# Normalizing the experts' mixture for eight tiles at a time, output gates carried in the record, second biases added while mixing

## The reference, cut to what matters

```python
xn = _layernorm(x)
# recurrent attention: 16 heads of 16 x 16 state
q, k = silu(xn @ Wq), l2_norm(silu(xn @ Wk)); v = xn @ Wv
f = sigmoid(xn @ Wf1 @ Wf2); a = k * (-sigmoid(xn @ Wgamma)) * f
for t in range(512):
    S = S * f_t; S = S + k_t * (a_t . S + v_t); o_t = q_t . S
o = o * sigmoid(xn @ Wog1 @ Wog2)          # the output gate
s = layernorm(o) * norm_w @ Wo
# experts: 2 of 8 for each token
y_e = gelu(xn @ W1[e] + b1[e]) @ W2[e] + b2[e]
g = silu(layernorm(sum_e cw[e] * y_e) * gamma + beta)
out = x + s * g
```

## Time and profile before

| | |
|---|---|
| median of 3 runs | 1239.27 us (1236.87 to 1240.11) |
| profiled execution, its own time | 1238.9 us |
| its span | 1237.2 us |
| busy: VectorE / TensorE / GpSimd / ScalarE | 90% / 76% / 74% / 32% |
| chain that ended last: GpSimd / VectorE / issue / TensorE / DMA | 36% / 27% / 16% / 7% / 6% |
| TensorE clock granted, mean | 0.869 of full speed |
| moved by DMA | 202.6 MB |

### The profile page before, as it was taken

The page is one execution under the profiler, slowest core; times in us unless marked ns, Lnnn a source line. Parts: engine busy times, 40 slices in busy tenths (PEclk is TensorE's granted clock), DMA queues, the critical chain, the costliest instruction groups (busy, mean ns, idle before and its releaser), DMA issues.

```text
span 1237.2 us, 17465 instructions
## 1 busy us (share of the span) xinstructions
PE 938.7 (76%) x3773; PEld 683.6 (55%) x3774; DVE 1119.4 (90%) x3502; ACT 395.7 (32%) x1047; POOL 918.9 (74%) x902
## 2 busy tenths in 40 slices
PE   5798898100029999999999999999999934667663
PEld 2343343000018888778888777888878723445441
DVE  3799999999999999999999999999999995988882
ACT  3444444200003333332232223333322203554552
POOL 3766666367844888888888888888888884877762
PEclk9888988655559999999999999999999976777787
DMA  5666656553335666655666556666666427355322
GB/s 165 194 209 177 213 180 188 140 191 107 111 94 150 191 196 195 195 170 183 191 195 193 174 177 195 196 187 181 183 192 191 120 67 210 93 157 149 99 81 69
DMA packets 247251, 202.60 MB, mean 164 GB/s; under 512 B 141425, under 2 KB 225233, under 8 KB 247185
## 3 DMA queue, kind: packets, MB, share of 16 engines
q1 hardware_dynamic: 170146, 82.81, 25.5%
q10 hardware_dynamic: 70224, 100.49, 24.8%
q0 software_dynamic: 6816, 18.69, 4.6%
HBM read 139.42 MB, written 62.54 MB: 163 GB/s over the span
## 4 chain that ended last, share of the span: by engine, by line
POOL 36%; DVE 27%; issue 16%; PE 7%; DMA 6%; SPq 3%; ACT 3%; POOLq 0%; DVEq 0%; ACTq 0%
POOL prod_q L327 13%; POOL prod_a L310 12%; POOL y_d L530 5%; DMA rec_d<-work 4%; DVE obh L1164 3%; PE psA L959 3%; DVE ubuf L1180 3%; DVE prod_a L1175 2%; PE psF L921 2%; SPq L335 2%; DVE prod_q L316 1%; DVE prod_a L1198 1%; DVE state L1204 1%; DVE outer L1190 1%; POOL cross L583 1%
## 5 line engine op out<-in xcount | busy, mean ns | idle before, releaser
L310 POOL TENSOR_TENSOR prod_a<-state,rbh 128x512 f32<-128x512 f32 x200 | 254.7, 1274 | 96.2 <-DVE state L1237 74.0
L903 PE MATMUL psF<-wts,work 128*128 128x256 f32 x1248 | 289.1, 385 | 3.2 <-ACT work L712 2.0
L891 PE MATMUL psA<-xgT,wts 128*128 128x256 f32 x1248 | 282.3, 384 | 0.9 <-ACT xgT L706 0.8
L891 PEld LDWEIGHTS psA<-xgT,wts 128*128 128x128 f32 x1248 | 235.4, 191 | 45.1 <-issue 13.8
L903 PEld LDWEIGHTS psF<-wts,work 128*128 128x128 f32 x1248 | 230.8, 190 | 50.0 <-issue 16.5
L327 POOL TENSOR_TENSOR prod_q<-state,rbh 128x512 f32<-128x512 f32 x175 | 223.2, 1276 | 0.0
L1164 DVE TENSOR_REDUCE obh<-prod_q 128x16 f32<-128x272 f32 x512 | 217.6, 426 | 0.0
L712 ACT ACTIVATE work<-psA,b_sb 128x256 f32<-128x256 f32 x312 | 130.8, 470 | 162.3 <-PE psA L891 159.5
L1224 DVE TENSOR_REDUCE ubuf<-prod_a 128x16 f32<-128x272 f32 x200 | 86.0, 430 | 37.5 <-POOL prod_a L310 37.1
L723 ACT ACTIVATE work<-psF,work 128x256 f32<-128x256 f32 x78 | 36.9, 473 | 256.9 <-PE psF L905 256.9
L879 PE MATMUL psT<-ident,work 128*128 128x128 f32 x156 | 24.2, 279 | 119.2 <-DMA work<-xs_d 119.1
(11 more groups left out here) (171 smaller groups left out, 1543.3 us busy)
## 6 DMA issues: line engine op xcount, KB each, us to landing
wts<-in_L_ffn_W_dram ACTq DMA_DIRECT2D x78, 1024.0 KB
rec_d<-work SPq DMA_DIRECT2D x32, 640.0 KB
rbh<-rec_d SPq DMA_DIRECT2D x32, 640.0 KB
xs_d<-zero SPq DMA_DIRECT2D x26, 387.0 KB, 9.0
work<-xs_d ACTq DMA_DIRECT2D x39, 258.0 KB
wts<-y_d ACTq DMA_DIRECT2D x16, 512.0 KB, 5.5
x_acc<-in_L_attn_x_dram SPq DMA_DIRECT2D x32, 128.0 KB
og_d<-work SPq DMA_DIRECT2D x32, 128.0 KB, 7.9
```

Source lines behind the costliest of these rows:

```text
L310: eng.tensor_tensor(prod_a[:, n, 1:3, :, 0:HD], state[:, g % SR, :, :].unsqueeze(1).broadcast_to(wide), rows.unsqueeze(2).broadcast_to(wid ...
L891: mm = pe.matmul(psA[m // 2 % 2][:, m % 2 * MT:(m % 2 + 1) * MT], w1_sb[v][:, c, m * P:(m + 1) * P], xgT[:, c, :], start=(c == 0), stop=(c ...
L903: pe.matmul(psF[q][:, 0:D], hT[:, m, q * P:(q + 1) * P], w2_sb[v][:, m, :], start=(m == 0), stop=False)
```

## The change

The record grows to 6 x 16 numbers: the output gate's sigmoids are written into it by one ScalarE instruction together with f. `og_d`, `ogs` and their DMAs go. A finished chunk of outputs is multiplied by its gates in `obh` (`gate_outputs`, 128x256): by VectorE for chunks 0 to 6 and 31, by GpSimd for chunks 7 to 30, behind pair 3 (GATED) of the next chunk; loads and stores of chunks wait for that. GpSimd's preparation moves from pairs 3 to 5 to pairs 4 to 6.

The b2 matmul leaves the expert tiles. Instead `route` forms each token's eight weights, TensorE turns them (into `cwT`), and `add_experts` begins each sum with a matmul of `cwT` and b2, which is held in four places (four small loads after a memset).

Mixing takes the moments of eight tile pairs ahead; `spreads` handles eight tiles (GQ) at once, four times in all, at places given by SPREADS; `moments` copies the sum to `x_acc`, so that the sum's PSUM is free before `normed`. ScalarE and TensorE finish the mixing of 24 tiles before the first output tile; the last eight alternate with output tiles 0 to 7. `out_scales` moves behind the next pair's products. LAND_STEP is 15.0 and PAIR_STEP 3.82.

```diff
-REC = 5 * HD
-A_, F_, K_, Q_, V_ = (HD * n for n in range(5))
+REC = 6 * HD
+A_, F_, O_, K_, Q_, V_ = (HD * n for n in range(6))
...
+GQ = 8
+SPREADS = (596.0, 608.0, 624.0, 650.0)
+GATED = 3
-LAND0, LAND_STEP = 390.0, 15.9
-PAIR_STEP = 3.7
+LAND0, LAND_STEP = 390.0, 15.0
+PAIR_STEP = 3.82
...
+        def gate_outputs(eng, c):
+            eng.tensor_tensor(obh[:, c % OB, :, :], obh[:, c % OB, :, :], rbh[:, c % RB, :, O_:O_ + HD], ALU.mult)\
+                .then_inc(s_og, 1)
...
-            sp.dma_start(b2_sb[:, :, :], b2.rearrange("(a e) n -> a e n", a=1)).then_inc(s_c, 16)
+            sp.wait_ge(s_pool0, 5)
+            for n in range(4):
+                sp.dma_start(b2_sb[n * E:(n + 1) * E, n, :], b2).then_inc(s_c, 16)
...
             def spill(n):
                 u4 = n % RS
-                sp.wait_ge(s_og, n + 1)
-                sp.dma_start(og_d[n], ogs[:, u4, :]).then_inc(s_ogd[u4], 16)
...
             def next_chunk(c):
-                sp.wait_ge(s_o, (c + 1) * RING)
+                sp.wait_ge(s_og, c + 1)
...
                 if n >= SL:
-                    sp.wait_ge(s_mul, n - SL + 1)
+                    sp.wait_ge(s_fb, n - SL + 1)
                 sp.dma_start(f_on[:, n % FR, :], o_r[n]).then_inc(s_fl[n % SL], 16)
-                sp.dma_start(fog[:, n % SL, :], og_d[n]).then_inc(s_fl[n % SL], 16)
...
-                if s % NP == 0:
+                if s % NP == GATED:
                     c = WOVEN + s // NP - 1
-                    sp.wait_ge(s_o, (c + 1) * RING)
+                    sp.wait_ge(s_og, c + 1)
...
-            def spreads(j):
-                lo, hi = 2 * j, 2 * j + 2
+            def spreads(q):
+                lo, hi = q * GQ, (q + 1) * GQ
...
-                if 3 <= g % NP < 6 and g // NP + 1 < NCH:
-                    prepare_part(g // NP + 1, g % NP - 3)
+                if g % NP == GATED and g // NP > SHARED:
+                    pool.wait_ge(s_o, g // NP * RING)
+                    gate_outputs(pool, g // NP - 1)
+                if 4 <= g % NP < 7 and g // NP + 1 < NCH:
+                    prepare_part(g // NP + 1, g % NP - 4)
                 s = g - WOVEN * NP
+                if spread < NT // GQ and ((g - SHARED * NP) * PAIR_STEP >= SPREADS[spread] or s >= 2):
+                    spreads(spread)
+                    spread += 1
                 if s >= 0:
                     for q, (lo, hi) in enumerate(NORMS):
-                        if s == hi - 1 and s < NT - 1:
+                        if s == hi:
                             out_scales(q)
...
-                    if s % 2 == 0:
-                        spreads(s // 2)
...
-                act.activation(rec[:, u4, :, F_:F_ + HD], heads(psF[u][:, 0:D]), ACT.Sigmoid).then_inc(s_f, 1)
-                act.activation(ogs[:, u4, :], psF[u][:, D:2 * D], ACT.Sigmoid).then_inc(s_og, 1)
+                act.activation(rec[:, u4, :, F_:F_ + 2 * HD].rearrange("p h (s c) -> p s h c", s=2),
+                               psF[u][:, :].rearrange("p (s h c) -> p s h c", s=2, h=H), ACT.Sigmoid).then_inc(s_f, 1)
...
-                    act.activation(junk[:, n % 2, :], summed(n), ACT.Copy, accum_out=ysum[:, n:n + 1]).then_inc(s_sum, 1)
+                    act.activation(x_acc[:, n, 0:D], summed(n), ACT.Copy, accum_out=ysum[:, n:n + 1]).then_inc(s_sum, 1)
...
-            moments(0)
-            for j in range(NT // 2):
-                normed(j)
...
+            half = GQ // 2
+            for j in range(2 * half):
+                moments(j)
+            for q in range(NT // GQ):
+                act.wait_ge(s_yr, q + 1)
+                for j in range(q * half, (q + 1) * half):
+                    normed(j)
+                for j in range((q + 2) * half, min((q + 3) * half, NT // 2)):
+                    moments(j)
+                for j in range(q * half, (q + 1) * half):
+                    silu_g(j)
+                    if q < NT // GQ - 1:
+                        if j > q * half:
+                            turned_back(j - 1)
+                    else:
+                        n = 2 * (j % half)
+                        out_normed(n)
+                        out_normed(n + 1)
+                        out_turned(n)
+                        turned_back(j)
+                        out_turned(n + 1)
+                if q < NT // GQ - 1:
+                    turned_back((q + 1) * half - 1)
+            for n in range(GQ, NT):
...
-                    pe.matmul(psF[q][:, 0:D], ones[0:1, :], b2_flat[:, bass.ds(e * D, D)], start=False, stop=True)\
-                        .then_inc(s_y, 1)
+                    mm.then_inc(s_y, 1)
...
                 if j >= 2:
-                    pe.wait_ge(s_yn, 2 * (j - 1))
+                    pe.wait_ge(s_sq, 2 * (j - 1))
                 for n in range(2 * j, 2 * j + 2):
+                    total = sums[j % 2][:, n % 2 * D:(n % 2 + 1) * D]
+                    pe.matmul(total, cwT[:, n // 4, :], b2_sb[:, n % 4, :], start=True, stop=False)
                     for c in range(2):
...
+                link(dve.tensor_tensor(gs[:, 2, :], gs[:, 2, :], gs[:, 0, :], ALU.mult))
+                dve.tensor_copy(x_acc[:, :, D], gs[:, 2, :]).then_inc(s_gate1, 1)
+                link(dve.tensor_tensor(pr, m1, over_e(2), ALU.mult))
+                link(dve.tensor_tensor(rest_, m2, over_e(4), ALU.mult))
+                dve.tensor_tensor(pr, pr, rest_, ALU.add).then_inc(s_cw, 1)
...
-                if out_tile is not None and out_tile < NT - 1:
-                    gate_o(out_tile)
...
+                    if n == GATED and 0 < c <= SHARED:
+                        dve.wait_ge(s_o, c * RING)
+                        gate_outputs(dve, c - 1)
```

More of the change, by code:

```diff
@@ L168, in build @@
         oTs = xTs
+        cwT = w_kq[0:4 * E, :, :].rearrange("p c n -> p (c n)").rearrange("p (n t) -> p n t", t=P)
         sel = gw[:, 0, :, :].rearrange("p t e -> p (t e)")
-        b2_flat = b2_sb[:, :, :].rearrange("a e n -> a (e n)")
         f_on = work[:, 0:FR * D].rearrange("p (u d) -> p u d", u=FR)
-        fog, fx, f_sg = (work[:, (FR + n * SL) * D:(FR + (n + 1) * SL) * D].rearrange("p (u d) -> p u d", u=SL)
-                         for n in range(3))
+        fx, f_sg = (work[:, (FR + n * SL) * D:(FR + (n + 1) * SL) * D].rearrange("p (u d) -> p u d", u=SL)
+                    for n in range(2))
         s_x = [sem(f"s_x{n}") for n in range(len(STATS))]
@@ L208, in build @@
         s_recd = [sem(f"s_recd{n}") for n in range(RS)]
-        s_ogd = [sem(f"s_ogd{n}") for n in range(RS)]
         s_gt = sem("s_gt")
@@ L220, in build @@
         s_b1t = sem("s_b1t")
+        s_cw = sem("s_cw")
+        s_cwT = sem("s_cwT")
+        s_cws = sem("s_cws")
         s_b1 = sem("s_b1")
@@ L398, in _ @@
                 sp.wait_ge(s_yd[u], 16 * MH * ((NM + 1 - u) // 2))
-            for u in range(RS):
-                sp.wait_ge(s_ogd[u], 16 * (NT // RS))
             def fetch(n):
@@ L591, in _ @@
             number(0)
-            landed = 0
+            landed = spread = 0
             for g in range(SHARED * NP, T // 2):
@@ L684, in _ @@
             act.wait_ge(s_b1, 1)
+            act.wait_ge(s_cwT, 1)
+            for n in range(2):
+                act.activation(cwT[:, 4 * n:4 * n + 4, :].rearrange("p n t -> p (n t)"), psA[n][0:4 * E, :], ACT.Copy)\
+                    .then_inc(s_cws, 1)
             act.wait_ge(s_slot, 2)
@@ L688, in _ @@
                 act.wait_ge(s_recd[u], 16 * (NT // RS))
-            for u in range(RS):
-                act.wait_ge(s_ogd[u], 16 * (NT // RS))
             def expert_of(t):
@@ L872, in _ @@
             pe.matmul(psT[1][:, 0:NT * E], ones[:, :], sel, start=True, stop=True).then_inc(s_cnt, 1)
+            pe.wait_ge(s_cw, 1)
+            for n in range(NT // 4):
+                mm = pe.transpose(psA[n // 4][0:4 * E, n % 4 * P:(n % 4 + 1) * P],
+                                  gw[:, 1, 4 * n:4 * n + 4, :].rearrange("p t e -> p (t e)"), ident[:, :])
+            mm.then_inc(s_cwT, 1)
             pe.wait_ge(s_slot, 2)
+            pe.wait_ge(s_cws, 2)
             def turn_rows(t, v, nth):
@@ L917, in add_experts @@
                 if j >= 2:
[L918 removed]
+                    pe.wait_ge(s_sq, 2 * (j - 1))
                 for n in range(2 * j, 2 * j + 2):
+                    total = sums[j % 2][:, n % 2 * D:(n % 2 + 1) * D]
+                    pe.matmul(total, cwT[:, n // 4, :], b2_sb[:, n % 4, :], start=True, stop=False)
                     for c in range(2):
[L921 to L922 removed]
+                        mm = pe.matmul(total, ident[:, :], yab[:, g % YR, c, n % GM, :], start=False, stop=(c == 1))
                 mm.then_inc(s_yab, 1)
@@ L960, in out_rows @@
                 mm.then_inc(s_s, 1)
-            add_experts(0)
-            for j in range(NT // 2):
-                if j + 1 < NT // 2:
-                    add_experts(j + 1)
-                turn_y(j)
-                turn_back(j)
-                if j > 0:
```

(16 more changed lines are left out.)

71 lines of the change are left out of this document (25 added, 46 removed).

## The result

The changed kernel takes 1296.65 us (median of four runs, 1295.98 to 1298.98), the kernel before 1239.69 beside it (1236.87 to 1241.72). The ratio is 1.046 (95% interval 1.044 to 1.049). The forecast had been 1221, range 1204 to 1238.

The account below looks back on a forecast made before the run. The recurrence's chain of waits between GpSimd and VectorE was taken as the bound. First sum at 978, plus 99 to tile 0, 111 and 5 of woven pairs, 26.5 tail and 1.7 around the span: 1221 us, range 1204 to 1238.

Parts of the forecast that it names:

- Front and experts: Stages before mixing: 57th pair 3 us later, expert tiles 14.9 us, pair pace 3.81 us, first sum at 978.
- A sum has 12 matmuls instead of 8: Mixing on TensorE: each tile pair's sum takes 2.8 us at 0.24 us per matmul, the first 4.4.
- rival B: Mixing: TensorE keeps the low clock, sums 5.4 us, tile 0 at 1122, end at 1266; chance 0.08.
- Turns: Mixing after the sums: silu, turn back and next turn take 2.7 us a tile pair at mean clock 0.70.
- seven spreads 4.8: VectorE's small operations for output groups in the woven pairs after tile 0: 0.7 us each, 4.8 in all.
- The 5 that I had left for late output tiles: Woven pairs: 5 us allowed for output tiles whose scales come just in time, bounds 0 and 16.
- one row of the front: Front gate products on VectorE: a 414 ns row taken to show no blocking by GpSimd; 2.4 us for seven.
- Waits: Woven stage: some 50 us of VectorE's waits can be had, including 17.1 us for gate tiles.
- a single wait at tile 0: VectorE, ready at 1060, waits 17 us for output tile 0, which comes at 1077.
- the tail: From the last state to the end: 26.5 us, against 27.1 before.

Follow-up runs that it names:

- e1: The changed kernel with the second-bias weights padded by zero rows from 32 to 128 rows; 1249.21 us, ratio 1.008 to the kernel before.
- e4: The changed kernel, 32-row bias weights kept, bias product first in even tiles and last in odd ones; 1257.95 us.
- e2: The changed kernel with the second-bias weights padded to 64 rows instead of 128; 1297.51 us.
- e9: e1 with output tiles started one group of eight sooner, output moments in PSUM and two-operand spread instructions reading one operand there; 1226.48 us, ratio 0.988.
- e10: e1 with GpSimd computing the output tiles' scales one pair earlier, as the kernel before does; 1243.04 us, ratio 1.003.
- e12: e9 with output tiles woven in from the seventh tile pair and the spread's last two all-SBUF operations reading one PSUM operand; 1211.87 us, ratio 0.975.

## Why the prediction was wrong, by its own steps

- **Front and experts: right in mechanism.** L905 has gone; the pace beside the experts is 154 pairs in 594 us from 386 on, 3.86 us (forecast 3.81). The last landing starts at 974.4 and the first sum at 982.7 (forecast 978). VectorE's waits for products there (386 to 960 us) are 22.3 us against 16.1 in the earlier trace rows: the densely placed landings cost somewhat more than I took.
- **The step that failed: "A sum has 12 matmuls instead of 8. At 0.24 us each (8 in 1.89) it takes 2.8 us."** It took 6.31. I priced the added products by a row of products whose weights are all 128 rows high, though the change makes them alternate with weights 32 rows high. The rows also held both ends, 1.89 and 3.62 for eight, and I kept the upper one only as rival B. The kernel before changes height too, around its second biases with weights of one row, and its weight loads stand idle there:

```profile
574.24 0.29 PEld L905 LDWEIGHTS psF<-b_sb,ones 1*128 1x128 f32 x2 [0.33 <-issue]
574.86 3.32 PEld L903 LDWEIGHTS psF<-wts,work 128*128 128x128 f32 x16 [0.33 <-issue]
```

So 0.62 us for two instructions, where two of 128 rows take 0.43 (e1), was a price on record. But it comes twice in 16 us and at a clock of 1.00, and nothing in it showed that the clock would stay low. The step is 15 x 3.5 = 52 us by itself; e1, in which only the heights are equal, has tile 0 49 us sooner.
- **Rival B had the place, not the cause.** B said 5.4 us a sum, tile 0 at 1122, end at 1266, with a chance of 0.08. The clock stayed low as B says, but I had it come from TensorE's rests, and argued it away with "TensorE would hardly rest while summing". It did not rest by the profile, 75.78 of 75.80 us, and the clock was 0.50. The Trainium skill (TensorE: Matmul & The Clock Gate, A second HAM failure mode: psum-queue depth-cycling) tells of a clock that goes back and forth where TensorE idles briefly between groups of matmuls. This trace agrees only in part: the weight loads idle 0.65 us at each change of height and e4, with half of the changes, has its high clock, but TensorE counts as busy and its clock doesn't go back and forth, it stays. The same page (Step-by-step: what each phase is for) says that the time of loading weights doesn't depend on the row count K. The traces agree: from 980 to 1100 us a load takes 308 ns with 32 rows and 324 with 128 in the changed kernel, 309 with 64 rows in e2. What alternating heights change is when a load begins.
- **Turns: "with the mean granted clock of 0.70 in this stretch 2.7 a tile pair".** Measured 3.63, 11 us in twelve tile pairs. The cycle was right, its clock wasn't: from 1059 to 1074 us the changed kernel has 0.50, where I took the mean of another stretch, and one cycle at the high clock takes 2.78 (e1). The 2.7 also leaves out ScalarE's copy back, 0.6 us in the cycle, so it is too low even for the high clock.
- **Spreads: "seven spreads 4.8".** The forecast counted 0.7 us a spread, as in the kernel before, and moved GpSimd's scale group behind the next pair's products without asking what those products now run beside. They run beside the spread, which took 2.75 to 3.30 us from its first start to its last end, against 0.78 before (1116.44 to 1117.22): 15 us in seven. The 5 that I had left for late output tiles, and that did not come, covered a part. The Trainium skill (SBUF — State Buffer, Who interferes with whom) has the rule, and the prediction weighed it against one row of the front and found it wanting. In the woven stage the traces agree with it: held until the end of GpSimd's instruction (1189.75 and 1189.74), free with a PSUM operand (e9), free when GpSimd is quiet (e10). It also bears on the two single-input operations of e9: the page names tensor_scalar among those that can take the ports shared with GpSimd, under conditions; here the two took 0.82 and 0.69 us from SBUF to SBUF and 0.16 in e12.
- **Waits: right.** Gate tiles 17.1 to 0, GpSimd's wait for variances to 3.0, a single wait at tile 0 (17 forecast, 23.1 found), the tail 26.8.
- **With the measured sizes in its terms** the sum would have been 1221 + 52 (sums) + 11 (turns) + 10 (spreads, less the 5 left free) + 5 (first sum) = 1299, against 1296.65. Sums and turns give 63 where the stretch has 60.1, and small terms are left out (power groups, waits), so the agreement to 2 us is partly luck.

## What to carry to other kernels

Before adding a small product to a stream of matmuls, look at the shape of its weights beside its neighbours': zero rows up to the neighbours' height cost next to nothing in the product (379 ns an instruction in e1 against 374 for 32 rows in e4, both at the high clock), and heights alternating at every tile cost 47 us here; if padding is impossible, order the products so that equal heights stand together. When a queue is reordered, ask not only who waits for the moved work but what now runs beside the other engine's operations, and look for operations of a few elements that take a microsecond. When work is added to fill an engine's idle time, look whether another engine waits for what stands behind it. When work is gathered ahead of a consumer, the whole gathered queue becomes the latency of its first item: start the consumer after as few items as its own inputs allow.

## What the runs showed of the hardware that was not expected

- Weights of 32 or 64 rows alternating with 128 at every tile: the weight load at each change idle 0.65 us, granted clock 0.50 for 75.8 us of unbroken business. That is 6.31 us a tile pair. Same products, bias products in neighbouring pairs (e4): 2.98 us and clock 1.00, each load beside a change idle 0.33 us. All 128 rows (e1): 2.6.
- A VectorE operation on 128x4 elements took up to 1.23 us (L1006 in e1, at 1122.21) beside GpSimd when all its operands lay in SBUF, and 0.15 to 0.17 with one in PSUM (e12).
- Five more products per tile pair on TensorE, 60 in all, raised its clock from 0.50 to 0.99 in the turns and left output tile 0 where it was (1094.0 against 1093.3 us), because two of the five stood in the chain between the engines, 0.87 us a cycle.
